# Carried scan states on four row tiles, a third bank for the input projection, second head's exponentials ahead of the output copies, both block diagonals on VectorE

## What is computed

```python
x = x + _L0_conv_ref(_gn(x), ...)      # local correlation and a 1x1 convolution
x = x + _L1_conv_ref(_gn(x), ...)      # gated selective scan
x = x + _L2_conv_ref(_gn(x), ...)      # 1x1 convolution
x = x + _L3_conv_ref(_gn(x), ...)      # 1x1 convolution
# L1: xz = silu(in_proj(x)); x_ssm, res, gate = split(xz); xf = silu(dwconv(x_ssm))
#     permute the 1024 tokens for each of 2 heads, then for every token t:
def step(h, inp):
    dA_t, dB_t, x_t, C_t = inp
    h = dA_t[:, :, None, :] * h + dB_t[:, :, None, :] * x_t[..., None]   # 256 x 8 state
    y_t = jnp.einsum('bhds,bhs->bhd', h, C_t)
    return (h, y_t)
#     permute back; y = y * silu(gate) + res; out = silu(out_proj(y))
```

## Time and profile before

| what | us |
|---|---|
| runs of the kernel before | 1723.71, 1725.22, 1725.95 (median 1725.22) |
| the profiled execution, its own time | 1724.77 |
| its span in the trace | 1722.9 |
| TensorE busy | 1637.4 (95%) |
| VectorE busy | 1169.0 (68%) |
| ScalarE busy | 890.2 (52%) |
| GpSimd busy | 402.6 (23%) |

### The profile page before, as it was taken

The page is one execution under the profiler, slowest core; times in us unless marked ns, Lnnn a source line. Parts: engine busy times, 40 slices in busy tenths (PEclk is TensorE's granted clock), DMA queues, the critical chain, the costliest instruction groups (busy, mean ns, idle before and its releaser), DMA issues.

```text
span 1722.9 us, 24375 instructions
## 1 busy us (share of the span) xinstructions
PE 1637.4 (95%) x8661; PEld 920.4 (53%) x8661; DVE 1169.0 (68%) x2480; ACT 890.2 (52%) x1091; POOL 402.6 (23%) x418
## 2 busy tenths in 40 slices
PE   4588999999999999999999999999999999999987
PEld 3254654556545655456545565455554565545643
DVE  6779776567755676548775578556775577653865
ACT  4647453475355653555544754457525564446532
POOL 1304311043021431223220430204302142113310
PEclk9789999999999999999999999999999999999999
DMA  6303410244102431224212441024310242112301
GB/s 206 99 0 105 147 28 14 74 134 143 41 23 84 126 119 41 75 73 147 76 22 74 129 147 28 17 78 142 128 40 34 85 138 96 39 49 79 113 12 49
DMA packets 140718, 140.17 MB, mean 81 GB/s; under 512 B 68899, under 2 KB 118115, under 8 KB 140590
## 3 DMA queue, kind: packets, MB, share of 16 engines
q1 hardware_dynamic: 126542, 103.18, 19.5%
q0 software_dynamic: 12288, 34.68, 6.2%
q10 hardware_dynamic: 1760, 0.64, 0.2%
HBM read 78.46 MB, written 60.01 MB: 80 GB/s over the span
## 4 chain that ended last, share of the span: by engine, by line
PE 82%; DVE 11%; issue 3%; ACT 3%; DMA 1%; POOL 0%; DVEq 0%; SPq 0%; POOLq 0%; ACTq 0%
PE bank L1632 77%; PE bank L1800 2%; PE bank L1933 2%; DVE bn L921 1%; DVE gate L1144 1%; PE bank L1852 1%; DVE scan_tmp L1504 1%; ACT L719 1%; DMA x_even<-in_x 1%; ACT work L573 1%; DVE wmax L891 0%; DVE work L1584 0%; ACT buf_a L570 0%; PE bank L1702 0%; DVE scan_tmp L1506 0%
## 5 line engine op out<-in xcount | busy, mean ns | idle before, releaser
L1632 PE MATMUL bank<-buf_a,win_hi 128*128 128x512 f16 x1536 | 460.7, 382 | 8.2 <-DVE buf_a L993 8.1
L1632 PE MATMUL bank<-buf_a,win_lo 128*128 128x512 f16 x768 | 292.5, 381 | 0.0
L1632 PE MATMUL bank<-buf_b,w_hi 128*128 128x512 f16 x960 | 286.7, 380 | 2.5 <-DVE buf_b L993 2.5
L1632 PEld LDWEIGHTS bank<-buf_a,win_hi 128*128 128x128 f16 x1536 | 148.5, 99 | 174.7 <-DVE buf_a L993 10.9
L471 POOL DMA_INDIRECT d_scan<-rows,rank x128 | 126.5, 988 | 347.2 <-ACT rows L654 304.6
L1632 PE MATMUL bank<-buf_b,w_lo 128*128 128x512 f16 x480 | 182.4, 380 | 0.0
L487 POOL DMA_INDIRECT rows<-d_y,rank x128 | 129.1, 1008 | 203.7 <-DMA d_y<-buf_b 168.2
L1632 PE MATMUL bank<-buf_a,w_hi 128*128 128x512 f16 x576 | 171.3, 379 | 2.2 <-DVE x_odd L1236 2.1
L1632 PEld LDWEIGHTS bank<-buf_b,w_hi 128*128 128x128 f16 x960 | 93.7, 99 | 111.9 <-DVE buf_b L993 3.2
L1632 PEld LDWEIGHTS bank<-buf_a,win_lo 128*128 128x128 f16 x768 | 75.5, 98 | 91.9 <-issue 2.2
L1632 PE MATMUL bank<-gate,w_out 128*128 128x512 f32 x256 | 120.3, 603 | 1.1 <-DVE gate L1349 1.1
(11 more groups left out here) (256 smaller groups left out, 3058.9 us busy)
## 6 DMA issues: line engine op xcount, KB each, us to landing
rows<-d_scan SPq DMA_DIRECT2D x16, 1024.0 KB, 5.9
d_y<-buf_b SPq DMA_DIRECT2D x64, 256.0 KB, 2.4
work<-in_x SPq DMA_DIRECT2D x24, 512.0 KB, 4.6
d_gram<-rows SPq DMA_DIRECT2D x32, 260.0 KB, 2.4
x_even<-in_x SPq DMA_DIRECT2D x16, 512.0 KB, 6.6
x_odd<-in_x SPq DMA_DIRECT2D x16, 512.0 KB, 5.5
out_x<-x_even SPq DMA_DIRECT2D x16, 512.0 KB, 2.9
out_x<-x_odd SPq DMA_DIRECT2D x16, 512.0 KB, 2.6
```

Source lines behind the costliest of these rows:

```text
L1632: return eng.matmul(out, lhsT, rhs, start=start, stop=stop, skip_group_check=True, **kw)
```

## The change

It does these things, in the scan and in the order around it:

- the state group isn't group 0 in each chunk, but group `4 * (c // 2)`, so that the rows of the state lie at partitions 0, 32, 64 and 96 for chunk pairs 0 to 3. `hst` lies there too, `gam` and `a_col` are on all partitions, and the masks `left`, `right` and the offsets are kept by chunk pair;
- the state columns of `pfac` are copied out to `p_far` by a small DVE product and then set to zero in `pfac`, so ScalarE's copy of `pT` needs no `keep`;
- a carried matmul uses only the 32 rows of its pair; `scan_y` now does four whole-chunk matmuls, then the carried ones of these chunks, half by half;
- all seven state products come in one run into bank 6, between the two halves of the inner products;
- the block diagonal of head 0 is made on VectorE too, and POOL's instruction is gone;
- ScalarE does the first two exponentials of head 1 ahead of all output copies of head 0;
- the last units of the input projection go round three banks (0, 1, 2), pieces are laid out anew, the spread of the bound goes directly behind the second `scan_y`, and the first output parts are in another order.

```diff
-FAR_GROUP = (0, 0)
+PAIRS = NT // 2
+far_group = lambda c: 4 * (c // 2)
@@ banks
-        yt_bank = ((3, 5), (4, 6), (3, 3), (4, 4))
-        dh_bank = lambda c: (3, 4, 0, 0)[c // 2]
-        m_bank = 5
+        yt_bank = ((5, 4), (3, 6), (3, 3), (4, 4))
+        dh_bank = 6
+        m_bank = 3
+        y_bank = (5, 3, 4, 6)
-        in_bank = (3, 4, 6, 1, 2, 1, 2, 1, 2, 1, 4, 5, 6, 3, 2, 1, 4) + (2, 1) * 3 + (2,)
-        out_bank = (0, 2, 1, 5, 6, 0, 3, 4)
+        in_bank = (3, 4, 6, 1, 2, 1, 2, 1, 2, 1, 4, 5, 6, 3, 2, 1, 4, 2, 0, 1, 2, 0, 1, 2)
+        out_bank = (0, 1, 2, 5, 6, 0, 3, 4)
@@ POOL
-                diagonal()
                 gather(0)
                 gather(1)
@@ ACT
                 scan_factors(0)
                 filler(2)
+                scan_exp(1, 0)
+                scan_exp(1, 1)
                 scan_y(0, 0)
-                scan_exp(1, 0)
                 scan_y(0, 1)
-                scan_exp(1, 1)
-                scan_y(0, 2)
                 scan_exp(1, 2)
                 scan_decays(1)
+                scan_y(0, 2)
                 scan_y(0, 3)
                 scan_factors(1)
-                filler(2)
+                filler(3)
                 for j in range(4):
                     scan_y(1, j)
                 filler(1)
                 y_high(m, 0)
                 y_high(m, 1)
                 filler(1)
                 y_high(m, 2)
-                filler(1)
                 y_high(m, 3)
@@ DVE scan_factors
                 wait(eng, "fac_exp", m, 3 * h + 1)
+                TT(p_far[:, :, :].rearrange("p (j b) s -> p j b s", b=2), far, wgt.rearrange("p (j b) s -> p j b s", b=2),
+                   ALU.mult).then_inc(s["fac_pq"], 1)
+                wait(eng, "fac_pq", m, 5 * h + 1)
+                eng.memset(far, 0.0).then_inc(s["fac_pq"], 1)
+                wait(eng, "fac_pq", m, 5 * h + 2)
                 TT(p4, p4, wgt.unsqueeze(2).broadcast_to([P, NT, G, S]), ALU.mult).then_inc(s["fac_pq"], 1)
@@ DVE scan_blocks
-                if h:
-                    wait(eng, "fac_8", m, 4 * h + 4)
-                    TT(diag.rearrange("p (c b t) -> p c b t", c=NT, t=T8),
+                wait(eng, "fac_8", m, 4 * h + 4)
+                TT(diag.rearrange("p (c b t) -> p c b t", c=NT, t=T8),
@@ DVE scan_states
-                        STT(hst[hp, c, :], hst[hp, c - 1, :], gam[:, h, c:c + 1], inc, ALU.mult, ALU.add).then_inc(s["h_st"], 1)
+                        STT(hst[hp(c), c, :], hst[hp(c - 1), c - 1, :], gam[hp(c - 1), h, c:c + 1], inc, ALU.mult, ALU.add).then_inc(s["h_st"], 1)
@@ PE
+                        elif q == 18:
+                            wait(eng, "sp_z", m, 1)
...
+                def state_products(h):
+
+                    wait(eng, f"scanx{h}", m, 16)
+                    for c in range(NT - 1):
+                        ins = mm(ps[dh_bank][32 * (c % 4):32 * (c % 4) + S, (c // 4) * DH:(c // 4 + 1) * DH],
+                                 p_far[:, c, :], rows4[:, h, c, 0:DH], True, True)
+                    ins.then_inc(s["dh_mm"], 1)
...
+                def bound_spread():
+
+                    wait(eng, "w_maxr", m, 2 * ROUNDS + 3)
+                    mm(bound_all, const("ones")[0:1, :], y_bound[0:1, 1:2], True, True).then_inc(s["w_maxb"], 1)
...
+                    def carried(c):
+
+                        rows_of_pair = slice(32 * (c // 2), 32 * (c // 2) + 32)
+                        return mm(out(c), qT[rows_of_pair, c * P:(c + 1) * P], hst[rows_of_pair, c - 1, :], False, True)
+
+                    for half in range(2):
+                        wait(eng, "m_ev", m, 2 * h + half + 1)
+                        if half:
+                            wait(eng, "h_st", m, 7 * h + 7)
+                        for c in range(4 * half, 4 * half + 4):
+                            mm(out(c), mmat[:, c * P:(c + 1) * P], r[:, c, 0:DH], c % 2 == 0, c == 0)
+                        if half and between:
+                            between()
+                        if half == 0:
+                            wait(eng, "h_st", m, 7 * h + 3)
+                        for c in ((1, 2, 3), (4, 6, 5, 7))[half]:
+                            ins = carried(c)
+                            if c % 2 == 1:
+                                ins.then_inc(s["y_mm"], 1)
+                        if half and behind:
+                            behind()
@@ PE order
                 scan_sums(0)
-                piece(6)
+                piece(7)
                 factor_rows(0, 0)
-                piece(2)
+                piece(1)
                 factor_rows(0, 1)
+                piece(1)
                 scan_inner(0)
                 scan_sums(1)
-                filler(1)
+                piece(3)
                 scan_y(0)
+                piece(3)
                 factor_rows(1, 0)
-                piece(2)
+                piece(1)
                 factor_rows(1, 1)
+                piece(1)
                 scan_inner(1)
-                piece(2)
-                scan_y(1, bound_across)
+                piece(5)
+                scan_y(1, bound_across, bound_spread)
@@ behind the scan
-                piece(4)
+                piece(2)
                 y_chunk(0, 0)
-                wait(eng, "w_maxr", m, 2 * ROUNDS + 3)
-                mm(bound_all, const("ones")[0:1, :], y_bound[0:1, 1:2], True, True).then_inc(s["w_maxb"], 1)
                 y_chunk(1, 0)
-                piece(4)
+                piece(2)
                 y_chunk(0, 1)
                 y_chunk(1, 1)
-                piece(4)
+                piece(2)
                 wait(eng, "in_evac", m, 23)
                 wait(eng, "y_lo", m, 1)
                 out_part(0, 0)
+                out_part(1, 0)
+                out_part(3, 0)
                 wait(eng, "in_evac", m, 24)
-                out_part(1, 0)
                 out_part(2, 0)
...
```

134 lines of the change are left out of this document (49 added, 85 removed).

## The result

The changed kernel takes 1714.5 us in the median of four runs (1712.75 to 1716.53), the kernel before 1725.0 beside it. The ratio is 0.9939, with a 95% interval of 0.9926 to 0.9952. It is faster by 10.5 us. I had forecast 1712 in a range of 1700 to 1722. The profiled execution took 1714.69, with a span of 1712.9.

What follows compares the result with a forecast made beforehand. TensorE, busy 95% of the span, was taken as the bound, with head 1's gathers late next. Six middle images at 1.4, 3.2 for the last and 1.0 for the first sum to 12.6 us off 1724.77: 1712, range 1700 to 1722.

Steps and rivals of the forecast that it cites:

- TensorE's lead: At head 1's first transposes TensorE was to arrive 3.2 us sooner, at 824.8 and not 828.04.
- The sums: Last matmul of `scan_sums` widens from 8 to 128 columns and loses a mode switch: 0.2 us an image.
- the wait of 1.1: TensorE's wait ahead of head 1's output products for VectorE's addition L1567 was to go, 1.1 us an image.
- Row tiles side by side: Carried matmuls on 32-row tiles run in parallel, 1.2 us a half; gain 0.6 a head, 1.3 an image.
- The bound taken from the column groups: Low bound for a carried half: two slots plus 0.2 for the mode, as in state products, 1.07 us.
- Gathers take back a part of the lead: Middle images: TensorE waits 1.4 and 0.5 us for head 1's gathers, so 1.3 to 1.4 of 3.2 is gained.
- the landing of 2.8: Head 1's fourth gather was taken to land 2.8 us after its start, and the eighth with the same 2.8.
- My sign of being wrong: Forecast wrong if no gather wait appears, states are late again, or VectorE's added 0.45 us delays the factors' transposes.
- VectorE's 0.45: Two new VectorE instructions ahead of both heads' weighting, 0.22 us each, add about 0.45 us a head.
- the first gate: First image: VectorE's late chain starts at this gate, some 1.2 us earlier than now; 1.0 taken as gain.
- The gathers don't hold: Rival, chance 0.12: stores land sooner, the 3.2 us lead counts in seven images, 23.4 us gained, 1701.
- Stores land later: Rival, chance 0.14: stores cost 1.4 us more, middle images gain nothing, first and last 4.2, 1720.6.
- Row tiles take turns: Rival, chance 0.14: no overlap of carried matmuls, 2.6 us more an image, middle images lose 1.2, 1733.

## Why the forecast came out as it did

**The terms of TensorE's lead, one by one.** In head 0 the output product goes from 6.48 to 5.88 (789.95 to 795.83), exactly the 5.9 forecast. In head 1 the gain is 0.9, for two small reasons that I had not priced: the product no longer starts out of a wait (its first two steps took 0.97 then, 0.87 elsewhere), and the group's way out costs nothing, because the spread of the bound follows it. The seven state products take 0.98 where I had 1.1. But inner products and states together fell only from 3.07 to 2.95 (800.82 to 803.77), so an image gains 0.25 there and not 0.4. The sums give 0.17 (1.06 and 1.17 become 1.03 each), where I had 0.2. With the wait of 1.1, the gains up to the last product are 0.6 + 0.9 + 0.25 + 0.17 + 1.1 = 3.0, as forecast. The last product ends 0.96 later than before (forecast 0.9), the last copy 1.56 later (forecast 1.3), and TensorE could be at head 1's transposes 3.3 earlier (forecast 3.2). This part of the working held.

**Row tiles side by side.** Shown, by the timeline and by the run with whole rows. The bound taken from the column groups was good: 1.06 for a half against a low bound of 1.07. The 0.1 that I added for weight loads of 128 columns wasn't there. In its place 0.1 to 0.2 go ahead of a group: the four whole matmuls take 1.82 ahead of the first one (807.01 to 808.83) and 1.92 ahead of head 0's second (792.84 to 794.76), and 1.73 with whole rows. So the 1.2 for a half was right in size and partly wrong in kind. On the drain at a change of mode, which the Trainium skill states (TensorEngine Tiling (Array Packing), Key Properties), the rows agree in kind. The carried group costs 0.2 over its two slots of 0.43 when whole matmuls follow, and nothing over them when a matmul with one row follows (0.85).

**Gathers take back a part of the lead.** Shown. The wait moved from L1567 to L1942 in every middle image, the total wait for gathers is 12.4, and moving two fill steps behind the release gains 10.4. In size I was off twice. For the first wait I had 1.4, and in the six middle images it is 1.35 to 2.18, 1.75 in the mean. The step that failed here is the landing of 2.8 from the earlier trace rows. It is that of one gather in one image. The fourth gathers of the six middle images of the kernel before landed in 2.8 to 3.9, 3.4 in the mean, and those of the changed kernel in 3.1 to 3.8, 3.3 in the mean. With 3.3 my own sum would have given a wait of 1.9. For the second half I had a further wait of 0.5, and there is none: TensorE comes to it 5.05 after the first half, the gathers take 5.16 for their four, and they land 0.6 sooner than the fourth did because the loads are through by then (2.7 to 3.2). So 1.9 in all was forecast to be handed back, and 1.75 was.

**Why a middle image gave 1.9 and not 1.4.** The stretch lines above split it. TensorE's busy time fell by 14.0 in the six images, 2.3 each, and its idle time rose from 8.0 to 10.7, 0.45 each. Forecast were 1.9 less busy (1.3 + 0.4 + 0.2) and 0.6 more idle (1.9 less 1.1 and 0.2). So nearly all of the surplus lies in matmul time. Counted from start to start over the six images, an image gained 1.53 in the output products (forecast 1.3), 0.24 in inner products and states (0.4) and 0.17 in the sums (0.2), which is the forecast's 1.9. The other 0.4 lies where I had priced nothing. Some 0.2 were the last matmul of the factors' transposes, which took 0.20 and not 0.11 directly ahead of the state products. Another 0.16 were the last fill matmul ahead of the old wait, and 0.1 the transposes that the spread of the bound used to interrupt.

**VectorE.** Head 0 stayed where it was, as argued from POOL's blocking, and undoing it changes nothing. Head 1's diagonal is 0.6 earlier and not 0.9. Its last addition ends at 807.91, 1.0 later than I forecast (807.6, with the 0.67 added 808.58), but TensorE takes it up only at 809.89. VectorE stands for 1.05 ahead of the states' copy for the state products, which end some 0.8 later than I had them. This was a miss without a price.

**First image: the step that failed.** I had it 1.0 shorter, and it is 2.1 longer. All positions here count from its `scan_masks`. My sign of being wrong, VectorE's 0.45 ahead of the transposes of the factors, did come: TensorE starts these at 11.99, before at 11.54. But the step that failed comes later. I took the first gate, 1.2 earlier, to set the chain behind it. The gate begins only 0.5 earlier (48.96 against 49.45), and what then decides is the statistics of the next image. They need its loads, which SP issues when the last output product is done. SP starts them at 48.5 and not 46.3, the last one lands at 58.18 and not 54.65, and VectorE, which had not waited for them before, now does. TensorE's step on these statistics comes behind it (210.02 is 58.20 behind the masks):

```profile
210.02 2.47 DVE L914 BATCH_NORM_STATS2 bn<-x_odd 128x6 f32<-128x512 f32 x4 [0.95 <-DMA x_odd<-in_x]
215.89 0.39 PE L1632 MATMUL bank<-st,cst 128*128 128x8 f32 x2 [2.39 <-DVE st L934]
```

This step stands at 64.07 and before at 63.49: 0.6 later and not 1.0 earlier, 1.6 of the 3.1. So the later output product, which I had priced for the gathers of the middle images, had a second price here that I put at nothing. It moves as it should in other runs: the same wait is 0.15 with two fill steps moved, 0 with three, and 1.78 with the loads behind the stores. The other 1.5 come behind 240 us and are clock. Two stretches, before and then changed:

```profile
160.00:180.00 20.00, 17.34 (x102) 13.00 (x103) 16.64 (x26) 12.47 (x17) 2.93 (x2) 0.91 0.30 86
240.00:260.00 20.00, 19.89 (x136) 12.87 (x134) 14.79 (x48) 9.16 (x8) 3.05 (x3) 1.00 0.31 60
```

```profile
160.00:180.00 20.00, 16.19 (x92) 11.96 (x93) 16.52 (x30) 11.07 (x14) 1.40 (x2) 0.83 0.25 71
240.00:260.00 20.00, 20.00 (x137) 13.81 (x138) 13.71 (x46) 9.17 (x8) 2.56 (x3) 0.91 0.28 58
```

In the second pair TensorE is busy nearly all the time in both, and still the mean clock is 0.91 instead of 1.00, behind a wait of 2.14 that both kernels have. The lower clock of the first pair lies ahead of the wait of 2.39, which takes it in except for what it adds to the output product's lateness.

**Last image: right up to the scan's end, then clock.** TensorE is 3.4 ahead at the transposes of head 1's second half (56.75 behind the masks, 60.15 before), against 3.2 forecast. Waits of 0.39 and 0.19 for gathers are in it, where I had none. Of the 3.4, 1.9 goes in the tail, where the order of work is untouched. The tail as a whole, before and then changed, and one of the stretches of the changed one:

```profile
1646.50:1722.90 76.40, 61.99 (x261) 27.76 (x259) 50.48 (x124) 25.09 (x24) 4.38 (x8) 0.97 0.07 28
```

```profile
1634.80:1712.90 78.10, 65.20 (x260) 28.81 (x258) 50.50 (x124) 24.72 (x24) 4.37 (x8) 0.93 0.07 28
1656.00:1664.00 8.00, 6.24 (x22) 2.70 (x23) 6.17 (x20) 5.09 (x5) 1.08 (x2) 0.79 0.00 0
```

The tail's waits, up to 2.3, are nearly the same in both kernels. Behind one of them the clock fell before, behind three of them now. The matmuls are as many and busy for 3.2 more. The loss itself is one of these falls: behind the first wait, of 1.77 in both kernels, the clock falls now and didn't before, and TensorE's next step that waits comes 1.76 later. Why it falls more often isn't settled. It isn't a matter of this kernel alone, as the tail has two falls with whole rows or the diagonal on GpSimd, and three with two fill steps moved. The first and the last image took 216.8 and 135.0 in the run of the changed kernel once more. So the last image's loss repeats. The fall at 240 us didn't, and of the first image's 2.1 over before 0.7 was left. I had priced no term at all for the clock. It costs about 3.4 of the lead, 1.5 in the first image and 1.9 in the last.

**Rivals.** "The gathers don't hold" fell, as the wait is there in every middle image. "Stores land later" fell: the first gather starts 3.6 to 4.9 behind the last copy, before it was 3.1 to 5.1. The fourth gathers don't land later after their start either, 3.3 in the mean against 3.4. Both are longer than the 2.8 that I had read. "Row tiles take turns" fell by the timeline.

**What the runs don't take apart.** Of the 10.5 the row tiles are 4.4, by the run with whole rows. That number holds a last image that came out 0.9 shorter with whole rows, with one fall of the clock fewer. The rest comes with the new order of work. The wait for L1567 was 9.3 in eight images and is gone in the run with whole rows too. Which of the moved steps removed it, and what the single run of state products and the new place of the state rows give by themselves, no run separates.

## What to carry to other kernels

When the bound engine gets shorter, look for the chain that it releases itself: here copy, store and gather start with TensorE's own last product, so 1.5 us an image less of matmuls were worth 0.5 in a middle image. Work that hides a chain must stand behind the instruction that releases it, so moving two fill steps across that instruction was worth as much as the whole change (10.4 against 10.5). When fill moves, check the in-order engine that copies it out: one step too few ahead of its place cost all of the gain and more (1724.0 against 1702.7).

## What the runs showed of the hardware that I had not expected

- The landing of an indirect gather depends on what else moves. In the last image, which has no loads, each takes 2.6 to 3.1. In the changed kernel's fourth image the first takes 5.8 and the fifth 2.7, as the loads run out. With the loads behind the stores the first takes 6.5. The stores weren't slowed by the loads. I had read one landing and taken it for all.
- A short wait can cost twice. Behind a wait of 2.1 the granted clock was 0.72 over 6 us, and such an image lost 1.6 more behind the wait than images whose clock didn't fall. It happened in some images and not in others with the same wait.
- Four row-tile products on two tiles take 0.85 in either order, and no time for leaving the mode shows if a matmul with one row comes next. Whole ones behind them show 0.2, and whole ones ahead of them 0.1 to 0.2.
- Loads of the next image that are issued behind the last output product can hold up its statistics: in the first image VectorE waited 0.95 for them where it hadn't before.
